# One transition of an attention and mixture-of-experts kernel: work of all engines in listed sequences instead of steps, low parts of the experts' weights on VectorE

## The reference

```python
qkv = einsum('bsh,oh->bso', x, w_qkv)        # 16 query heads, 4 key/value heads, D = 128
q, k = layernorm(q, g, b), layernorm(k, g, b) # per head, then rotary embedding
weights = softmax(where(causal, -inf, q @ k.T / sqrt(D)))
attn_out = (weights @ v) @ w_o.T
...
weights, indices = top_k(softmax(xf @ gate_w.T), 2)   # 8 experts, 2048 tokens
out  = sum over the 2 chosen experts of weight * (silu(xf @ w_gate) * (xf @ w_up)) @ w_down   # H = 176
sh   = (silu(xf @ shw_gate) * (xf @ shw_up)) @ shw_down                                       # HS = 352
out += sigmoid(xf @ shgate_w) * sh
```

## Time and profile before

| | us |
|---|---|
| median of three runs | 704.52 (703.60 to 704.94) |
| the profiled execution | 706.78 |
| its span | 704.70 |
| busy, TensorE matmul / VectorE / ScalarE / GpSimd | 627.9 / 568.2 / 566.3 / 567.0 |
| first scatter, end of the last head's low part, last output projection copied | 486.35, 525.54, 529.80 |
| first matmul of a routed tile | 579.97 |
| TensorE busy without a gap from there | to about 660 |

### The profile page before, as it was taken

How to read it: one execution, slowest core, us unless ns; L and a number is a source line. 1 busy time by engine, 2 the same in 40 slices (tenths; PEclk the granted TensorE clock), 3 DMA queues, 4 the chain that set the end, 5 groups by cost and what they waited for, 6 DMA issues and landing times.

```text
span 704.7 us, 15492 instructions
## 1 busy us (share of the span) xinstructions
PE 627.9 (89%) x4412; PEld 581.1 (82%) x4412; DVE 568.2 (81%) x1921; ACT 566.3 (80%) x2177; POOL 567.0 (80%) x599
## 2 busy tenths in 40 slices
PE   3669999999999999999999999998668789999960
PEld 2457899999999999999999998897667679999960
DVE  6899999898988989889898899999456575555476
ACT  5689999999999989999999998998655356666543
POOL 5799899999999999999999999998854324665565
PEclk9699999999999999999999999999999899999995
DMA  8001205997530000000000000003222243443263
GB/s 338 2 1 32 74 27 173 334 335 184 4 43 1 2 1 2 1 2 1 1 2 1 2 1 2 1 24 103 109 84 85 90 121 100 121 127 121 71 238 113
DMA packets 50834, 54.20 MB, mean 77 GB/s; under 512 B 19808, under 2 KB 42336, under 8 KB 50624
## 3 DMA queue, kind: packets, MB, share of 16 engines
q1 hardware_dynamic: 47344, 43.84, 21.8%
q0 software_dynamic: 3408, 9.38, 3.6%
HBM read 23.76 MB, written 29.51 MB: 76 GB/s over the span
## 4 chain that ended last, share of the span: by engine, by line
POOL 53%; PE 23%; ACT 9%; DVE 6%; issue 5%; another core or an unknown queue 1%; DMA 1%; SPq 0%; ACTq 0%; POOLq 0%; DVEq 0%
POOL ropes L1736 11%; POOL ropes L1746 11%; POOL ropes L1739 10%; POOL rs L1724 9%; POOL hrow L1760 3%; PE pQ L458 2%; POOL osb L1767 2%; PE pQ L460 2%; PE pQ L459 2%; ACT ropes L867 2%; POOL rs L1722 2%; ACT P L882 2%; POOL lr L1724 2%; PE pO L458 1%; ACT P L890 1%
## 5 line engine op out<-in xcount | busy, mean ns | idle before, releaser
L458 PE MATMUL pQ<-W 128*128 128x512 f32 (+2 forms) x334 | 119.1, 357 | 11.1 <-DVE W L1193 5.3
L882 ACT ACTIVATE P<-P,nmx 128x128 f32<-128x128 f32 (+1 forms) x256 | 120.2, 502 | 0.0
L459 PE MATMUL pQ<-W 128*128 128x512 f32 (+2 forms) x334 | 114.3, 342 | 0.0
L460 PE MATMUL pQ<-W 128*128 128x512 f32 (+2 forms) x334 | 113.9, 341 | 0.0
L890 ACT ACTIVATE P<-P,rinv 128x128 f32<-128x128 f32 (+1 forms) x256 | 107.2, 491 | 1.6 <-DVE rinv L1266 1.2
L458 PE MATMUL pO<-W 128*128 128x256 f32 (+1 forms) x323 | 95.9, 297 | 13.8 <-DVE W L1275 7.8
L1736 POOL TENSOR_TENSOR ropes<-ropes 128x640 f32<-128x640 f32 x63 | 99.3, 1576 | 6.6 <-DVE ropes L1239 6.6
L1746 POOL TENSOR_TENSOR ropes<-ropes 128x640 f32<-128x640 f32 x63 | 99.8, 1584 | 4.9
L867 ACT ACTIVATE ropes<-pQ 128x128 f32<-128x128 f32 x320 | 89.8, 311 | 14.6 <-POOL ropes L1746 12.3
L1270 DVE TENSOR_TENSOR W<-pP,W 128x384 fp32r<-128x384 f32 x128 | 70.2, 549 | 30.6 <-ACT W L895 28.5
L459 PE MATMUL pO<-W 128*128 128x256 f32 (+1 forms) x323 | 91.8, 284 | 0.0
(11 more groups left out here) (242 smaller groups left out, 2227.1 us busy)
## 6 DMA issues: line engine op xcount, KB each, us to landing
xs<-stage SPq DMA_DIRECT2D x1, 17550.0 KB, 58.4
stage<-xs SPq DMA_DIRECT2D x39, 130.0 KB
ropes<-in_ew SPq DMA_DIRECT2D x8, 608.0 KB
stage<-in_wqkv SPq DMA_DIRECT2D x3, 768.0 KB, 8.7
stage<-ys SPq DMA_DIRECT2D x4, 512.0 KB, 7.2
ropes<-ys SPq DMA_DIRECT2D x4, 512.0 KB, 8.3
out<-X SPq DMA_DIRECT2D x8, 256.0 KB, 2.0
X<-in_wo SPq DMA_DIRECT2D x1, 1536.0 KB, 13.1
```

What stands on the lines that cost most here:

```text
L458: e.matmul(out, lh, rh, start=start, stop=False, skip_group_check=True)
L459: e.matmul(out, lh, rl, start=False, stop=False, skip_group_check=True)
L460: return e.matmul(out, ll, rh, start=False, stop=stop, skip_group_check=True)
L882: a = e.activation(P[:, z, span(t)], P[:, z, span(t)], ACT.Exp, bias=nmx[:, z, t:t + 1], scale=-1.0, accum_out=sums[:, z, t:t + 1])
```

## The change

In every engine the loop over steps now ends with step 128 (`WOVEN = 129`). From there to the first routed tile each engine issues a written-out sequence of calls, given below; then the loop over q goes on from the second routed tile. The tables and the `if q == ...` lines of the transition are gone. The calls are the same ones, with these differences. All eight low parts of the experts' weights are made on VectorE (ew_lo of GpSimd is gone), with one semaphore. The places of chunks 1 and 2 and the counts are written in the bank of the scores of odd heads (pS[1]), not in pA. Several waits are changed as the diff shows. The workspace of the last routing chunk has its own columns.

```diff
-S6 = 125
...
-EHI = {133: 0, 136: 1, 138: 2, 140: 3, 142: 4, 144: 5, 146: 6, 148: 7}
-ELO_D = {143: 4, 147: 5, 148: 6, 149: 7}
-EHALF = {137: 0, 140: 1, 142: 2, 143: 3, 145: 4, 147: 5, 148: 6, 149: 7}
+WOVEN = 129
...
-SWHI = [120, 121, 131]
+SWHI = [120, 121]
...
-            r = part(stage, 14 * RW, 2 * RW) if c == 0 else part(ropes, 3648, 312)
+            r = part(stage, 14 * RW, 2 * RW) if c == 0 else part(ropes, (3648, 3848)[c - 1], 48 * n + 8)
...
-                for (a, b) in CHUNKS for p in (pA,)]
-        pCnt = pA[:, 480:488]
+                for (a, b), p in zip(CHUNKS, (pA, pS[1], pS[1]))]
+        pCnt = pS[1][:, 480:488]
...
         def wait_ewlo(e, x):
...
+            e.wait_ge(s_ewlo, x + 1)
...
             else:
+                e.wait_ge(s_oproj, NHEAD)
                 e.wait_ge(s_pv, NHEAD // 2)
...
-                if b == NB - 1:
-                    e.wait_ge(s_placed, 2)
...
             def u_up(m):
                 if m == 0:
-                    e.wait_ge(s_max, NHEAD)
-                elif m == UFIRST:
-                    e.wait_ge(s_hUlo, m + 1)
-                else:
+                    e.wait_ge(s_max, NHEAD - 1)
+                    e.wait_ge(s_swlo, len(SWPART))
+                elif m != UFIRST:
                     e.wait_ge(s_uact, m)
+                e.wait_ge(s_hUlo, m + 1)
...
-                e.wait_ge(s_aT, min(COUNT_PV[c], NHEAD // 2))
-                if c == LASTC:
-                    e.wait_ge(s_logit, NB)
+                if c == 0:
+                    e.wait_ge(s_aT, COUNT_PV)
+                elif c == 1:
+                    e.wait_ge(s_max, NHEAD)
+                else:
+                    e.wait_ge(s_placed, 2)
...
             def u_rows_hi(m):
...
                 if m >= 4:
+                    e.wait_ge(s_ugate, m - 3)
                     e.wait_ge(s_uup, m - 3)
...
-                    elif c == 2:
-                        e.wait_ge(s_wdiff, c)
...
             def tile_ends():
                 k = 5 * len(CHUNKS)
+                e.wait_ge(s_cnt, 1)
...
-            for s in range(STEPS):
+            for s in range(WOVEN):
...
-            def ew_lo(x):
-                e.wait_ge(s_ewhi, x + 1)
-                e.tensor_tensor(ew[x][:, ELO:EW], ew_raw[x % 3][:, 0:EB], f(ew[x][:, 0:EB]),
-                                ALU.subtract).then_inc(s_ewlo_p, 1)
```

More of the change, by code:

```diff
@@ L765, in ffn @@
                     u_rows(i + 1)
-                if before2 == "U":
+                if before2 == "U" and q > U1:
                     u_down(g)
-                if before == "U":
+                if before == "U" and q > U1:
                     u_T(h)
[L770 to L774, removed]
                 if kind == "U":
@@ L814, in _ @@
                     logits(fb)
[L815 to L818, removed]
-                if s in COUNT and s < U0:
-                    places(COUNT[s])
-                ffn(s)
-            for q in range(STEPS, SEND):
+                if s == COUNT0:
+                    places(0)
+            scores(121)
+            qk_T(62, 0)
+            out_proj(115)
+            pv(58)
+            probs_T(118)
@@ new lines, in _ @@
+            scores(122)
+            out_proj(116)
+            out_proj(117)
+            probs_T(119)
+            scores(123)
+            qk_T(62, 1)
+            pv(59)
+            probs_T(120)
+            qk_T(63, 0)
+            probs_T(121)
+            ln2_T(6)
+            qk_T(63, 1)
+            scores(124)
+            scores(125)
+            logits(6)
+            out_proj(118)
+            out_proj(119)
+            pv(60)
+            u_rows(0)
+            u_rows(1)
+            probs_T(122)
@@ new lines, in _ @@
+            scores(126)
+            out_proj(120)
+            probs_T(123)
+            scores(127)
+            out_proj(121)
+            pv(61)
+            probs_T(124)
+            u_rows(2)
+            u_rows(3)
+            u_gate(0)
+            probs_T(125)
+            u_up(0)
+            out_proj(122)
+            out_proj(123)
+            u_rows(4)
+            u_rows(5)
+            places(1)
+            pv(62)
+            probs_T(126)
+            u_gate(1)
+            u_rows(6)
@@ new lines, in _ @@
+            u_up(1)
+            probs_T(127)
+            out_proj(124)
+            out_proj(125)
+            u_rows(7)
+            pv(63)
+            u_up(2)
+            u_T(0)
+            u_gate(2)
+            out_proj(126)
+            out_proj(127)
+            u_rows(8)
+            u_T(1)
+            u_up(3)
+            u_down(0)
+            u_T(2)
+            u_gate(3)
+            u_down(1)
+            u_gate(4)
+            u_up(4)
+            u_gate(5)
+            u_up(5)
@@ new lines, in _ @@
+            u_rows(9)
+            u_rows(10)
+            u_gate(6)
+            u_T(3)
+            ln2_T(7)
+            u_down(2)
+            u_T(4)
+            logits(7)
+            u_up(6)
+            u_T(5)
+            u_gate(7)
+            u_down(3)
+            u_gate(8)
+            places(2)
+            counts()
+            u_down(4)
+            u_T(6)
+            u_up(7)
+            u_down(5)
+            u_up(8)
+            u_down(6)
+            u_T(7)
+            u_gate(9)
@@ L823, in _ @@
+            u_up(9)
+            u_T(8)
+            u_gate(10)
+            u_up(10)
+            u_down(7)
+            u_T(9)
+            x_T(0)
+            u_down(8)
+            u_T(10)
+            x_T(1)
+            r_up(0)
+            u_down(9)
+            u_down(10)
+            for q in range(R0 + 1, SEND):
                 ffn(q)
@@ new lines, in _ @@
+            ew_lo(3)
+            pv_lo(63)
+            ew_lo(4)
+            u_lo(0)
+            u_rows_lo(6)
+            u_act(2)
+            out_stats(7)
+            u_lo(1)
+            ew_half(5)
+            ew_lo(5)
+            ew_half(6)
+            ew_lo(6)
+            u_act(3)
+            out_scale(7)
+            ew_half(7)
+            out_add(7)
+            ln2_stats(7)
+            u_act(4)
+            u_rows_lo(7)
+            u_rows_lo(8)
+            ew_lo(7)
+            u_lo(2)
@@ new lines, in _ @@
+            u_rows_lo(9)
+            u_act(5)
+            u_lo(3)
+            ln2_lo(7)
+            u_lo(4)
+            logit(7)
+            route_first_choice(2)
+            u_rows_lo(10)
+            route_second_choice(2)
+            route_gap(2)
+            route_count(2)
+            u_lo(5)
+            u_act(6)
+            place_read(2)
+            place_own(2)
+            place_ends(2)
+            tile_ends()
+            u_act(7)
+            u_lo(6)
+            tile_list()
@@ L1715, in _ @@
+            u_act(8)
+            u_lo(7)
+            shared_half(1, 14, NT)
+            u_act(9)
+            u_lo(8)
+            u_act(10)
+            u_lo(9)
+            x_lo(0)
+            u_lo(10)
+            x_lo(1)
+            r_act(0)
+            for q in range(R0 + 1, SEND):
                 ffn(q)
```

411 lines of the change are left out of this document (251 added, 160 removed).

## The result

| | kernel before | kernel after | ratio, 95% interval |
|---|---|---|---|
| first set of runs (9 and 9) | 705.72 | **701.66** | 0.9932 [0.9912, 0.9952] |
| second set of after, another occasion | 695.63 | 684.75 | 0.9834 [0.9809, 0.9859] |
| third set of after | 705.16 | 700.72 | 0.9949 [0.9934, 0.9964] |

What follows compares the result with a forecast made beforehand. A chain of single operations, each queued behind other work of its engine, was taken to bound the stretch before the first routed tile. 1.8 + 10.5 - 1.1 - 1.7 = 9.5 us, so 706.8 becomes 697.3 (median 695.0); range 687.5 to 703.5.

Steps and rivals of the forecast that it cites:

- The likeliest case: The forecast itself, a gain of 9.5 us (7 to 13), given a chance of 0.55.
- Part A: From 482 us to the last head's output: pv_lo(63) 0.9 us later at 526.4, last projection at 528.0, gain 1.8.
- those 4.3 us: ScalarE's idle time without a named releaser (3.3 and 1.0 us) up to the last head, kept unchanged; bounds 0 and 7.4.
- rival 2: Larger gain, 16 us (688.5): ScalarE's unnamed waits do not come back and neighbours are ready; chance 0.12.
- Rival 3: Slower, 711 us: casts and low parts pulled into the attention's tail lengthen the heads' serial loop; chance 0.1.
- Part B: From the last projection to the first routed matmul: the chain takes 39.7 us instead of 50.2, gain 10.5.
- the 2.0 of unnamed waits: Between last projection and first routed tile: ScalarE's waits without a releaser, 2.0 us added out of 3.1 seen.
- the 1.1 of u_down(9): Nine matmuls moved behind the first routed tile's r_up(0), taking 1.1 us back from the gain.
- The 1.7 for late neighbours: Estimated loss of 1.7 us for orders where one late neighbour holds the next; bounds 0 and 4.0.
- Rival 1: Half the gain, 4.0 us (700.5): load 6 lands late, so ScalarE's expert casts delay out_scale(7) by 5.5 us; chance 0.2.
- 4: The change does nothing, 704 us, because the stretch ends with a transfer that is not moved; chance 0.03.
- The rule that spoke against the change: Four low parts moved to VectorE and GpSimd's scatters could lock each other out, up to 3.8 us; forecast took nothing.

Runs made afterwards that it cites:

- 696 occasion: Two of the study's five sets of runs, in which the unchanged kernel before took 695.6 to 695.9 us.
- 706 occasion: The other sets of runs, in which the unchanged kernel before took 705.2 to 706.5 us.
- q3: Kernel before, with its scatters of chunks 0 and 1 held on GpSimd in pairs by waits; 697.02 us against 705.16, 0.989.
- q1: Kernel after, with each scatter of chunks 0 and 1 held on GpSimd to go out singly; 687.77 us against 705.16 for the kernel before, 0.9762.
- q2: Kernel after, with all twenty scatters of chunk 0 in one run; 706.18 us against 705.16 for the kernel before, 1.0003.
- e1: Kernel after, with the low parts of experts 0 to 2 back on GpSimd between the scatters; 698.43 us against 706.54 for the kernel before, 0.9897.
- e8: Kernel after, with all twenty scatters of chunk 0 in one run; 685.37 us against 695.94 for the kernel before, 0.9852.
- e5: Kernel after, with the load of expert 3's weights held until the cast of head 123's probabilities; 701.4 us, 0.9934 of the kernel before.

## Why the prediction was wrong, step by step

**The sign was right, the size was not**: 4.8 us by the ratio for 9.5. The likeliest case was the wrong one of those listed; the time, 701.66, lies inside the range, at its slow end.

**Part A is the step that failed**, by its own mark (pv_lo(63) after 530). Forecast were 526.4 for it and 528.0 for the projection's copy; 535.64 and 537.52 were measured. The term that was mis-sized is "those 4.3 us": I kept the unnamed waits of ScalarE at 4.3 (bounds 0 and 7.4) "since the list does not remove whatever made them". They measured 14.0, nearly twice the upper bound. 14.0 less 4.3 is 9.7, and pv_lo(63) was 9.2 late: this one term is all of it. The bound itself was read too low: the trace of before has 12.1 us of such waits of ScalarE in all, with 0.8, 1.7 and 2.3 beside the three that I took. And the list did touch what makes them. The low part that I read for its 2.25 us on GpSimd also stood between two runs of scatters, and so did the low part of the shared weights, which the list moved ahead of them. In rival 2 I even wrote that chunk 0's scatters go out without a break, and drew no bound from it.

The other terms of part A held within 2 us. Without unnamed waits, pv_lo(63) ended at 520.28 and the copy started at 522.16; the sum without its 4.3 gives 522.1 and 523.7. The wait for expert 0's load was 0.94 where 2.0 was taken. The 2.1 us for handovers stood on no row, and no run measures it alone. Rival 3, that the pulled-in blocks lengthen the heads' loop, would have shown there: pv_lo(63) came 1.9 us earlier than before (522.19), not later.

**Part B was better than forecast**: 35.5 us instead of 39.7. From the start of the copy, with forecast in brackets: out_scale(7) 6.1 (6.0), normalising begins 11.3 (11.0), last scatter 25.8 (26.1), first load 29.2 (31.7), first routed matmul 35.5 (37.7 and 2.0 for unnamed waits). The walk along the lists was right within 0.5 us up to the last scatter. Two terms fell away: the 2.0 of unnamed waits (none came), and 2.1 us between the last scatter and the first load, 3.5 where the earlier trace rows have 5.6. Behind that, two misses nearly cancel, which is luck: 3.3 us from the first load to its transpose for the 4.6 forecast, and 3.0 from there to the routed matmul for 1.4. A likely reason, not tested: before, the eighth expert's load was still under way then (issued at about 563), after, it had been issued at 537.

**Given back**: 1.9 us behind the first routed matmul for the 1.1 of u_down(9), on the 696 occasion 0.2; what makes that difference is open. The 1.7 for late neighbours was not needed.

**What the change is worth without the waits.** On the 696 occasion 10.9 us (695.63 to 684.75). In the two traces the copy of the projection comes 4.3 us earlier (526.48 and 522.16) and part B takes 8.7 less (43.7 and 35.0). That is 2 us more than the medians give; the profiled execution of before, 697.63, was 2.0 above 695.63. On the 706 occasion, with the scatters of both kernels spaced, 9.2 us (q3 697.02, q1 687.77). The forecast's 9.5 lies between these two, in part by luck: the copy gained 4.3 for the 1.8 of part A, and part B gave 8.7 for 10.5. The result was smaller because the waits in the heads' part grew from 5.1 to 14.0 us; those that before has in part B (1.7, 3.1 and 2.3) went.

**The rivals.** Rival 1 has the measured size (4.0) and not its mechanism: the casts of experts 5 and 6 ran back to back without a wait, the loads were there. Rival 2 named the condition of the 696 occasion, but put its gain against a kernel before that keeps its own waits; they go from both, so it is 10.9 and not 16. Rival 3 and 4 did not occur.

**The rule that spoke against the change.** I went by the row (a low part of 1.15 us while scatters were issued), for nothing; by the rule of the Trainium skill, page SBUF — State Buffer, section Who interferes with whom, up to 3.8 us was at stake. The rows after:

```profile
533.88 1.16 DVE L1477 TENSOR_TENSOR W<-ropes,W 128x960 fp32r<-128x960 f32 x1
...
533.99 1.89 POOL L2054 DMA_INDIRECT xs<-stage,slots  x1 [0.30 <-issue]
...
535.56 1.15 DVE L1477 TENSOR_TENSOR W<-ropes,W 128x960 fp32r<-128x960 f32 x1
...
536.18 1.37 POOL L2054 DMA_INDIRECT xs<-stage,slots  x1 [0.30 <-issue]
...
540.45 1.16 DVE L1477 TENSOR_TENSOR W<-ropes,W 128x960 fp32r<-128x960 f32 x1
...
540.56 1.64 POOL L1951 TENSOR_TENSOR lr<-lr,half 128x2 f32<-128x2 f32 x1
...
542.10 1.16 DVE L1477 TENSOR_TENSOR W<-ropes,W 128x960 fp32r<-128x960 f32 x1
...
542.40 1.80 POOL L2054 DMA_INDIRECT xs<-stage,slots  x1 [0.20 <-issue]
```

A scatter that comes up 0.1 us behind the start of a low part takes 1.89 instead of 0.96, the root's second step 1.64 instead of 0.72. Each is longer by about what was left of the low part when it started (0.93, 0.41, 0.92 and 0.84 us for 1.05, 0.53, 1.05 and 0.86). VectorE's 1.15 does not change. The row that I went by could not have shown it: a scatter (545.52) was under way when that low part began, and the next one (546.78) came up only 0.09 us before it ended. But the trace of before shows the lock in another place, which I overlooked: GpSimd's low part began at 513.81 for 2.24 us, and a VectorE operation of two SBUF inputs (L1418, 128x32) that began at 514.63 took 1.47 us, in other traces 0.18 to 0.23. By that section the order of issue decides who is blocked; this trace agrees where the low part came first, with 3.1 us by which these four GpSimd operations are lengthened. Where a scatter came first, it held nothing: the low part of 545.72 took its 1.15. The four cost nothing on the chain (out_scale(7) came 0.1 us off the forecast), for VectorE's list was the later one there.

## What to carry to other kernels

Before an engine's work is taken away or moved, look at what it separated: the low parts were load on GpSimd and also the breaks in a run of indirect DMAs. Idle time without a named releaser is a term with a cause; as long as that is not found, its upper bound is not what was seen once, and what runs unbroken beside it is the first suspect. Repeat both kernels on another occasion before a small gain is judged: the same change was worth 0.5%, 0.7% and 1.7%.

## What the runs showed of the hardware

- While GpSimd issues indirect DMAs of 128 rows without a break (one every 1.27 us), ScalarE can see the end of a TensorE operation up to 11.9 us late (500.66 to 512.58 in q2). In the traces only instructions that wait for TensorE are hit, once on VectorE (1.1 us, before, at 554.39); handovers between the other engines stay at some 0.05 us (after: ScalarE's cast ended at 506.35, VectorE began at 506.38). Runs of at most five among the heads, with gaps of mostly 0.8 us or more (q1, q3) or other work of GpSimd (e1, q3) between them, had none. On two of five occasions it did not occur at all, with 26 in a row (e8). What delays the signals is open: holding a load back (e5) changed nothing, and the instruction queues moved a packet at 500 us and the next at 523, while the waits ended at 505.86 and 517.14 (after).
- TensorE pays twice for such a wait. In the window with the 9 us of it the granted clock was 0.66 and in the next one 0.86, between the two levels of 1.2 and 2.4 GHz, where the same windows had 1.00 on the 696 occasion.
